# A bias row written into PSUM by ScalarE in place of a TensorE product, in a GNN kernel on one core

## The reference

```python
# L0: messages over 9375 edges, then a GRU cell
m   = relu(concat(h[src], edge_attr) @ W1.T + b1) @ W2.T + b2
agg = segment_sum(m, dst)
gi, gh = agg @ W_ih.T + b_ih, h @ W_hh.T + b_hh        # thirds: r, z, n
r = sigmoid(i_r + h_r);  z = sigmoid(i_z + h_z)
n = tanh(i_n + r * h_n)
h_new = (1 - z) * n + z * h                            # then batch norm, residual, layer norm
# L1: a gated relational layer, twice, over 10000 edges
w   = einsum('rb,bio->rio', att, basis)                # 30 bases, 2 relations
agg = segment_sum(sigmoid(x_j @ gate_w[r]) * x_j @ w[r], row)
out = agg + x @ root + bias                            # relu after the first of the two
```

## Time and profile before

| what | value |
|---|---|
| median of 3 runs | 503.72 us (501.85 to 504.39) |
| the profiled execution's own time | 501.35 us |
| its span (first to last instruction) | 499.6 us |
| granted TensorE clock, mean | 0.99 of full |
| DMA traffic | 121.20 MB, 243 GB/s |

### The profile page before, as it was taken

How to read it: one execution, slowest core, us unless ns; L and a number is a source line. 1 busy time by engine, 2 the same in 40 slices (tenths; PEclk the granted TensorE clock), 3 DMA queues, 4 the chain that set the end, 5 groups by cost and what they waited for, 6 DMA issues and landing times.

```text
span 499.6 us, 6648 instructions
## 1 busy us (share of the span) xinstructions
PE 471.7 (94%) x2231; PEld 300.6 (60%) x2231; DVE 293.6 (59%) x571; ACT 194.0 (39%) x347; POOL 99.9 (20%) x115
## 2 busy tenths in 40 slices
PE   7989859999999999899999999999799999999995
PEld 2434325544554545777666765684566688788884
DVE  5887748989898989456103379767123115542313
ACT  1878763443334433363216222764223004242000
POOL 0000535667666640000000060000000060000000
PEclk9999979999999999999999999999999999999998
DMA  8959895778777863969978899687997550200011
GB/s 249 426 216 380 300 351 167 258 239 267 243 262 237 266 217 106 407 241 358 394 282 319 337 300 336 268 338 315 387 387 278 212 169 1 84 1 1 21 43 43
DMA packets 29207, 121.20 MB, mean 243 GB/s; under 512 B 4283, under 2 KB 7307, under 8 KB 24687
## 3 DMA queue, kind: packets, MB, share of 16 engines
q1 hardware_dynamic: 17518, 92.33, 48.1%
q0 software_dynamic: 7856, 24.91, 16.4%
q10 hardware_dynamic: 3792, 3.43, 2.3%
HBM read 113.85 MB, written 6.82 MB: 242 GB/s over the span
## 4 chain that ended last, share of the span: by engine, by line
PE 76%; DMA 11%; DVE 6%; ACT 2%; issue 2%; DVEq 1%; another core or an unknown queue 1%; SPq 0%
PE ps L1350 16%; PE ps L1245 14%; PE ps L1406 12%; DMA basis<-in_basis 11%; PE ps L1444 9%; PE ps L1210 9%; PE ps L1291 5%; PE ps L1292 4%; PE ps L1389 3%; ACT CT L633 2%; PE ps L1176 1%; PE ps L1235 1%; DVE X L880 1%; PE ps L1188 1%
## 5 line engine op out<-in xcount | busy, mean ns | idle before, releaser
L660 ACT ACTIVATE rhi<-x 128x512 fp32r<-128x512 f32 x79 | 47.1, 631 | 71.0 <-DVE x L937 44.7
L1245 PE MATMUL ps<-X 128*128 128x512 f32 x158 | 74.7, 614 | 0.0
L1210 PE MATMUL ps<-basis,sel 128*32 128x512 f32 x496 | 57.6, 596 | 5.4 <-DMA basis<-in_basis 5.4
L591 POOL DMA_INDIRECT X<-u_rows,esrc x40 | 42.6, 1064 | 80.8 <-DMA u_rows<-X 52.9
L600 POOL DMA_DIRECT2D X<-w_layer x32 | 16.8, 651 | 208.3 <-DMA w_layer<-ev 104.4
L944 DVE SCALAR_TENSOR_TENSOR rlo<-x,rhi 128x512 fp32r<-128x512 f32 x79 | 50.8, 684 | 2.0 <-ACT rhi L660 2.0
L1444 PE MATMUL ps<-Xr,CT_r 128*128 128x512 f32 x200 | 47.0, 389 | 0.0
L1245 PEld LDWEIGHTS ps<-X 128*128 128x128 f32 x158 | 29.3, 196 | 28.7 <-issue 28.5
L591 POOL DMA_INDIRECT x_sb<-u_rows,esrc x39 | 40.3, 1033 | 18.8 <-issue 10.2
L1444 PEld LDWEIGHTS ps<-Xr,CT_r 128*128 128x128 f32 x200 | 37.5, 188 | 7.8
L1083 DVE SCALAR_TENSOR_TENSOR Xr<-ps,gate,Xr 128x512 fp32r<-128x512 f32 x20 | 14.9, 750 | 43.5 <-ACT Xr L748 43.5
(11 more groups left out here) (214 smaller groups left out, 748.5 us busy)
## 6 DMA issues: line engine op xcount, KB each, us to landing
basis<-in_basis SPq DMA_DIRECT2D x29, 2048.0 KB
X<-in_eaT SPq DMA_DIRECT2D x20, 256.0 KB
basis<-in_basis SPq DMA_DIRECT2D x8, 512.0 KB
X<-w_layer POOLq DMA_DIRECT2D x32, 128.0 KB, 3.0
w_layer<-ev SPq DMA_DIRECT2D x13, 256.0 KB, 10.5
X<-in_WhhT SPq DMA_DIRECT2D x3, 1024.0 KB, 13.6
basis_apart<-in_basis SPq DMA_DIRECT2D x1, 2048.0 KB, 19.8
X<-in_WihT SPq DMA_DIRECT2D x2, 1024.0 KB, 10.3
```

What stands on the lines that cost most here:

```text
L591: nc.gpsimd.indirect_dma_start(gat[e % GATHERS], None, t["u"][:, :], bass.IndirectOffsetOnAxis(ap=esrc[:, e:e + 1], axis=0)).then_inc(gat_ ...
L660: nc.scalar.activation(rhi[:, u % 2, s], pre[:, s], ACT.Relu).then_inc(hi_ready, 1)
L1210: mm = pe.matmul(bank[32 * g:32 * g + 32], sel[:, layer, s], held[:, g, s2], start=(s == 0), stop=(s == 3), tile_position=(0, 32 * g))
L1245: pe.matmul(ps[:, EA_BANKS[s]], eaT[:, u % 2, s * P:(s + 1) * P], W1bT, start=True, stop=True).then_inc(ea_done, 1)
```

## The change

ScalarE writes the bias row of the `hn`, `in` and `out` jobs (20 in all) into the job's bank before TensorE starts it, and TensorE's first product of the job adds to what stands there. The `r` and `z` jobs and the source rows of L0 keep their bias product.

The row comes from a new tile of 128 x 512, `bias_row`, which lies over the second half of `bias` (used last by the source rows). SyncE loads one row of the input, broadcast to all 128 partitions (256 KB written), four times: for `hn`, `in`, the first and the second layer. The first load is ahead of the list. The others stand in SyncE's list at the names `hn4`, `in4` and `out04`; each waits until ScalarE has written all five banks with the row before.

```diff
-PICK_GATE = {"r": 0, "z": 1, "in": 2, "hn": 3}
+PICK_GATE = {"r": 0, "z": 1}
+AHEAD = 2
+BIAS_CHANGES = (("hn", NT - 1), ("in", NT - 1), ("out", 0, NT - 1))
+BIAS_ROWS = ((66, 0), (64, 0), (32, 1), (64, 1))
...
+            def load_bias_row(i):
+                part, which = BIAS_ROWS[i]
+                sp.dma_start(bias_row, t["bias"][part:part + 1, which].broadcast_to([P, H])).then_inc(bias_row_in, 16)
+            sp.wait_ge(u_acc, NT)
+            load_bias_row(0)
             nb = SLOTS * (EARLY + 1)
             for name, _ in jobs.list:
+                if name in BIAS_CHANGES:
+                    i = BIAS_CHANGES.index(name) + 1
+                    sp.wait_ge(bias_in_bank, i * NT)
+                    load_bias_row(i)
...
+            def bias_into_bank(name):
+                n = jobs.biased.index(name)
+                act.wait_ge(bias_row_in, 16 * (n // NT + 1))
+                drained_by(act, jobs.list[jobs.at[name] - 8][0])
+                nc.scalar.copy(ps[:, jobs.bank(name)], bias_row).then_inc(bias_in_bank, 1)
...
                     ins.then_inc(upper_ready, 1)
+                if turn + AHEAD < len(jobs.list) and jobs.list[turn + AHEAD][0] in jobs.biased:
+                    bias_into_bank(jobs.list[turn + AHEAD][0])
...
-                    add_bias(bank, 0, PICK_GATE[kind])
+                    if kind in PICK_GATE:
+                        add_bias(bank, 0, PICK_GATE[kind])
+                    else:
+                        pe.wait_ge(bias_in_bank, jobs.biased.index(name) + 1)
...
-                    add_bias(bank, 1, PICK_LAYER[layer])
+                    pe.wait_ge(bias_in_bank, jobs.biased.index(name) + 1)
                     products(bank, m, root_hi, root_lo, start=False)
```

More of the change, by code:

```diff
@@ L82 @@
 PICKS = 4
-PICK_GATE = {"r": 0, "z": 1, "in": 2, "hn": 3}
-PICK_SOURCE, PICK_LAYER = 0, (1, 2)
+PICK_GATE = {"r": 0, "z": 1}
+PICK_SOURCE = 0
+AHEAD = 2
+BIAS_CHANGES = (("hn", NT - 1), ("in", NT - 1), ("out", 0, NT - 1))
+BIAS_ROWS = ((66, 0), (64, 0), (32, 1), (64, 1))
 SLOTS = 2
@@ L159, in __init__ @@
         self.upper = {name: n + 1 for n, name in enumerate(split)}
+        self.biased = [name for name, _ in self.list if name[0] in ("hn", "in", "out")]
+        assert all(self.list[self.at[name] - 8][0][0] != "agg" for name in self.biased)
     def bank(self, name):
@@ L263, in gnn_kernel @@
         dump = [part.rearrange("p (k n) -> p k n", k=KT) for part in (W2T[:, 3], iota[:].bitcast(F32)[:, 0:H])]
+        with nc.sbuf_tensor("bias_rows", [P, 2, H], F32) as bias_rows:
+            pass
         bias = sb("bias", [P, 2, H], F32R)
+        bias_row = bias_rows[:, 1]
         bias_raw = x1[:, 0:2]
@@ L337, in gnn_kernel @@
         bias_ready = sem("bias_ready")
+        bias_row_in = sem("bias_row_in")
+        bias_in_bank = sem("bias_in_bank")
         b2_parts = sem("b2_parts")
@@ L699, in split_w @@
                 nc.scalar.copy(w_hi[:, r], w_raw[:, r]).then_inc(w_hi_ready, 1)
+            def bias_into_bank(name):
[3 more added lines that the diff above has]
+                nc.scalar.copy(ps[:, jobs.bank(name)], bias_row).then_inc(bias_in_bank, 1)
             nw = EARLY
-            for name, e in jobs.list:
+            for turn, (name, e) in enumerate(jobs.list):
                 kind = name[0]
@@ L1350, in products @@
                     mm = pe.matmul(bank, a[:, k, m * P:(m + 1) * P], w[:, k], start=(start and i == 0),
-                                   stop=(stop and i == len(terms) - 1))
+                                   stop=(stop and i == len(terms) - 1), skip_group_check=not start)
                 return mm
@@ L1406, in _ @@
                             mm = pe.matmul(bank, a[k][:, m * P:(m + 1) * P], w[:, k], start=False,
-                                           stop=(i == parts[-1] and j == len(terms) - 1))
+                                           stop=(i == parts[-1] and j == len(terms) - 1),
+                                           skip_group_check=(kind not in PICK_GATE))
                 elif kind == "w":
@@ L1444, in sources @@
                                 mm = pe.matmul(bank, counts[:, n, r * NP + m * P:r * NP + (m + 1) * P],
-                                               half[n][:, r].bitcast(dt), start=False, stop=last)
+                                               half[n][:, r].bitcast(dt), start=False, stop=last,
+                                               skip_group_check=True)
                         mm.then_inc(bank_full, 1)
```

## The result

| | before | changed |
|---|---|---|
| median of 6 runs each, us | 502.84 | 508.37 |
| profiled execution, us (span) | 501.35 (499.6) | 507.46 (505.7) |
| first bias product of r0 to the end of the span, us | 274.2 | 280.9 |

A forecast was written before the change was run, and what follows sets the result against it. PE (TensorE) was taken as the bound, busy in 94% of the span. Terms + 5.5 (in0), + 2.5 (clock), - 0.9, - 0.6, + 2.3, - 1.6 gave + 7.2: 503.72 to 510.9 us, range 506.9 to 514.0.

The forecast's parts named there:

- What goes: On TensorE in hn, in and out jobs: 20 bias products go at 0.227 us each, 4.54 us in all.
- What comes on ACT: On ScalarE: 20 writes of 0.60 us, 12 us in all, with 16 of the 20 covered by TensorE's other work.
- in0's row: Ahead of in0: the row lands 10.4 us after issue, behind SyncE's pair; TensorE stands 6.9 us, in0 + 5.5 us.
- rival A: At in0: row lands early, 3.2 us as on an idle queue, no stand or half clock; - 0.9, 502.9 us, chance 0.08.
- The clock: Behind the stand at in0: the granted clock is at half for about 5 us, + 2.5 us (ends 0 and 3.5).
- in1 to in4, and the wait in w(1,1): After in0: four bias products saved, - 0.9 us, and the 0.63 us wait for a `basis` piece goes, - 0.6 us.
- out02 to out04: At these three jobs: only short transposes lie ahead, so TensorE waits for each write; 3 x 0.77, + 2.3 us.
- The other `out` jobs: At out00, out01 and layer 2's five: bias products saved without waits, 7 x 0.227, - 1.6 us.
- Sum: Whole kernel: all terms together + 7.2 us, 508.6 us for the profiled execution and 510.9 us for the median.
- D: Stand and clock as forecast, but out02 to out04 covered by weight loads ahead; + 4.2, 507.9 us, chance 0.07.
- E: At in0: row later still, 13.6 us after issue, or half clock for longer; + 10.3, 514.0 us, chance 0.10.

The follow-up runs named there:

- k3: The changed kernel with the row of `in` loaded by ScalarE's own DMA queue in place of SyncE's; ratio to the kernel before 1.0158.
- k7: The changed kernel with the row of `in` in a tile of its own, loaded 50 us ahead; ratio to the kernel before 0.9989.
- k10: The changed kernel with 28 extra TensorE products ahead of in0's wait for its row; ratio to the kernel before 1.0093.
- k2: The changed kernel with the bias rows of out02 to out04 written three jobs ahead instead of two; ratio to the kernel before 1.0078.
- k11: k9 with 10 extra TensorE products between the two halves of w(1,4); ratio to the kernel before 0.9875.
- k8: k7 with the bias rows of out02 to out04 written three jobs ahead, as in k2; ratio to the kernel before 0.9936.
- k4: The changed kernel with 20 extra TensorE products ahead of in0's wait for its row; ratio to the kernel before 1.0116.
- k1: The changed kernel with the five `in` jobs' bias products back on TensorE; ratio to the kernel before 1.0026.
- k9: k8 with the first layer's row loaded later, at the second xT job instead of in4; ratio to the kernel before 0.9912.

## Why the prediction was right, step by step

- **What goes.** 0.227 us a product was too little. Layer 2's `out` jobs are 7.25 us apart and were 7.52, so each is worth 0.27: a bias product costs not only its own step but 0.04 us behind it. In all 5.4 us, where I had 4.5 with 0.7 more as the upper end.
- **What comes on ACT.** Right. A write takes 592 ns in the middle (577 to 597), all 20 add 10 us to ScalarE's busy time, and 16 of 20 were covered.
- **in0's row.** The size was right: issued at 274.15 (I had 275.1 on a start 0.5 us later), landed after 10.7 (I had 10.4), a stand of 6.8 us (6.9), in0 + 5.2 (5.5). The reason was right in part. The packets of the row did come behind the pair. But I also had it that without that place in SyncE's ring the sum would be rival A's, and that was wrong: k3 took the row out of the ring, and the landing took 11.0 us. The trace had only loads behind a pair on the same queue and loads with nothing ahead, so it could not tell the ring from the load on the engines, and I should have said so. That 10.4 came so near to 10.7 is partly luck: SyncE was at the two pieces ahead of `bn` from 348.75 to 353.63, at those ahead of the row for 2 us. The way out was not another queue but another time and place (k7).
- **The clock.** Forecast + 2.5, measured 2.3 (k10 against the change).
- **in1 to in4, and the wait in w(1,1).** - 0.9 and - 0.6; of these, in2 to in4 and the wait lie between w(1,0) and z1: - 1.3 forecast there, - 1.6 measured (7.33 to 5.70). Right in size, and the wait went; that GpSimd's loads coming earlier against the piece is the reason, no run tests.
- **out02 to out04.** Forecast + 2.3, measured + 2.5 (5.42 to 7.94), a wait of 0.83 us each; k2 got back 3.3.
- **The other `out` jobs.** - 1.6 forecast. Seven at 0.27 are 1.9.
- **Sum.** + 7.2 forecast; 6.6 in the list of the trace, 6.1 in the profiled execution, 5.3 (3.9 to 6.6) by the ratio. The terms of gain that I had at 0.227 make most of the difference in the list. The rest I can't assign: executions differ by several us in the stage ahead, and in whether the clock falls behind a basis wait. Two sums of the prediction are slightly off by their own terms: D less 0.7 is 507.2, not 506.9, as the lower end of the range, and E is + 10.4, not + 10.3.
- **Rival A** was wrong for this kernel, as the row landed late, but k7 is the case that it describes, with the row in time and the rest as changed. It had - 0.9 there, with a longer wait in w(1,1) and the loss at out02 to out04. k7's list time is - 0.1: the wait is 1.13 us (from 0.63), out02 to out04 lose their 0.83 us each, and the fall of the clock behind w(1,4), 1.6 us, is what A did not have.

## What to carry to other kernels

Work that is moved off the busiest engine brings its operands with it: ask when the last reader of the tile that they are loaded into is done, and what transfers are in flight then, on any queue. "Two jobs ahead" is a time only if the job in between is long; count the shortest one. And where the busiest engine waits 2 us or more, price the clock behind the wait beside the wait itself; filling the gap with products into a bank that is free let in0 start within 0.3 us of its time (k10) and saved a fall of 2.3 us there, of which 1.2 us then went into a later wait for DMA. At w(1,4), where such a fall costs 1.6 us, a filled gap is in the fastest kernel (k11), but one trace does not show that it kept the clock.

## What the runs showed of the hardware

- A load of 256 KB in 2 KB pieces took 10.7 us to land with 4 MB in flight on its own queue, and 11.0 us from another queue (k3); with nothing ahead the same kind took 3.2, and the shortest landing of the changed kernel's four rows is 3.6 us. The row loaded at in4 took 18.9 (k8) and 19.6 us (k7): it has a pair and a store ahead of it too, and GpSimd's 16 loads of 128 KB are under way at the same time. Nothing waits for it there, but at in0 it would have meant a longer stand.
- The granted clock fell behind idle times of TensorE of 6.8 to 7.2 us (in all three traces that have one: the change, k2, k3), of 2.46 us (k4), and of 2.6 to 2.85 us at w(1,4) in five of ten traces (k1, k4, k7, k8, k9), and did not in the other five, with waits of the same length. It cost 2.3 us in the first case and about 1.6 in the last (k8, over w(1,4): - 2.17 to - 0.54). So it can be one reason why single executions of one kernel differ, but the stage ahead of the list differs by more, 7.2 us over the twelve traces.
- ScalarE's write of 128 x 512 into PSUM (592 ns in the middle) takes about as long as its copies, casts and activations of the same size out of it (group means of 582 to 598 ns in the kernel before), and a product without `start` adds to what ScalarE wrote, in banks whose last products had covered all 512 columns.
